# GpSimd's share of the square roots: a shorter iteration, and 40 pieces in place of 16

## The reference

```python
xn = _layernorm(x)
q2, k2 = sum(q * q), sum(k * k)
d2 = maximum(q2[..., :, None] + k2[..., None, :] - 2.0 * einsum('bhid,bhjd->bhij', q, k), 1e-12)
attn = softmax(-sqrt(d2), axis=-1)
out = einsum('bhij,bhjd->bhid', attn, v) @ wo.T + bo
```

## Time and profile before

| | |
|---|---|
| median of 3 runs | 1478.79 us (1478.11 to 1479.42) |
| profiled execution, its time | 1478.12 us |
| its span | 1476.4 us |
| ScalarE busy | 1445.5 us, 98% |
| VectorE busy | 1245.1 us, 84% |
| TensorE busy with matmuls | 1124.6 us, 76% |
| GpSimd busy | 632.1 us, 43% |
| mean granted TensorE clock | 0.935 |

### The profile page before, as it was taken

How to read it: one execution, slowest core, us unless ns; L and a number is a source line. 1 busy time by engine, 2 the same in 40 slices (tenths; PEclk the granted TensorE clock), 3 DMA queues, 4 the chain that set the end, 5 groups by cost and what they waited for, 6 DMA issues and landing times.

```text
span 1476.4 us, 21636 instructions
## 1 busy us (share of the span) xinstructions
PE 1124.6 (76%) x7910; PEld 439.8 (30%) x7910; DVE 1245.1 (84%) x2236; ACT 1445.5 (98%) x795; POOL 632.1 (43%) x529
## 2 busy tenths in 40 slices
PE   5587786887887988878879774787777677776766
PEld 2122223244242442442424410232123123221212
DVE  7897888988989889789798787858898898998886
ACT  4999999999999999999999999999999999999998
POOL 5166460755509577595685820732113024022200
PEclk8598888999999999999999997999999999999899
DMA  4842644223232212122121321034033133021020
GB/s 130 242 143 56 171 128 124 53 58 85 79 136 65 55 43 53 43 54 62 35 66 43 89 68 31 19 108 93 28 113 78 29 111 84 27 101 39 22 70 20
DMA packets 104062, 112.73 MB, mean 76 GB/s; under 512 B 41723, under 2 KB 76027, under 8 KB 103947
## 3 DMA queue, kind: packets, MB, share of 16 engines
q1 hardware_dynamic: 98618, 99.47, 24.8%
q0 software_dynamic: 4464, 11.09, 2.7%
q10 hardware_dynamic: 864, 0.69, 0.2%
HBM read 66.52 MB, written 44.70 MB: 75 GB/s over the span
## 4 chain that ended last, share of the span: by engine, by line
ACT 64%; DVE 13%; issue 13%; PE 7%; POOL 2%; DMA 1%; SPq 0%; DVEq 0%; ACTq 0%; POOLq 0%
ACT scores L776 25%; ACT scores L746 22%; ACT exp L1295 11%; DVE scores L695 6%; DVE exp L1303 4%; PE pvb L676 3%; ACT exp L1291 2%; PE ring L661 1%; ACT ht L1028 1%; ACT L776 1%; POOL yro L1082 1%; ACT L746 1%; PE ring L1270 1%; PE ring L989 1%; POOL at L1245 0%
## 5 line engine op out<-in xcount | busy, mean ns | idle before, releaser
L695 DVE TENSOR_SCALAR scores<-ring 128x1024 f32<-128x1024 f32 x512 | 589.2, 1212 | 27.3 <-PE ring L661 27.1
L776 ACT ACTIVATE scores<-scores 128x8192 f32<-128x8192 f32 x63 | 438.9, 7020 | 0.2
L1295 ACT ACTIVATE exp<-ring 128x1024 f32<-128x1024 f32 x438 | 432.6, 1416 | 0.2
L746 ACT ACTIVATE scores<-scores 128x8192 f32<-128x8192 f32 (+1 forms) x60 | 411.2, 6921 | 2.7 <-DVE scores L695 2.5
L1270 PE MATMUL ring<-stk 128*128 128x512 bf16 x1024 | 306.8, 386 | 122.1 <-ACT exp L1295 102.5
L676 PE MATMUL pvb<-scores,val 128*9 128x256 f32 x4096 | 325.2, 393 | 82.7 <-issue 39.1
L1303 DVE SCALAR_TENSOR_TENSOR exp<-exp 128x512 f32<-128x512 f32 x438 | 322.3, 757 | 61.0 <-ACT exp L1295 56.6
L661 PE MATMUL ring<-stk 64*128 64x512 bf16 x1024 | 209.9, 407 | 55.0 <-DVE scores L695 44.0
L1270 PEld LDWEIGHTS ring<-stk 128*128 128x128 bf16 x1024 | 65.8, 97 | 337.6 <-ACT exp L1295 240.5
L661 PEld LDWEIGHTS ring<-stk 64*128 64x128 bf16 x1024 | 49.8, 93 | 286.2 <-DVE scores L695 205.4
L676 PEld LDWEIGHTS pvb<-scores,val 128*9 128x9 f32 x4096 | 66.1, 89 | 213.3 <-issue 210.5
(11 more groups left out here) (262 smaller groups left out, 1402.8 us busy)
## 6 DMA issues: line engine op xcount, KB each, us to landing
stk<-stack SPq DMA_DIRECT2D x192, 192.0 KB, 2.9
stack<-qp SPq DMA_DIRECT2D x7, 768.0 KB, 4.6
stack<-kp SPq DMA_DIRECT2D x7, 768.0 KB, 5.6
xj<-xg SPq DMA_DIRECT2D x10, 448.0 KB
yg<-xj POOLq DMA_DIRECT2D x10, 448.0 KB, 3.6
stack<-qp SPq DMA_DIRECT2D x7, 512.0 KB, 5.2
stack<-kp SPq DMA_DIRECT2D x7, 512.0 KB, 5.1
stk<-sum_rows SPq DMA_DIRECT2D x128, 24.0 KB
```

The source lines that it names most:

```text
L695: nc.vector.tensor_scalar(S[place][:, j * N:(j + 1) * N], tile, 1e-12, None, ALU.max).then_inc(o.release(("qk", group, place, j)), 1)
L746: nc.scalar.activation(part, part, ACT.Sqrt).then_inc(root_done, 1)
L776: nc.scalar.activation(S[place][:], S[place][:], ACT.Exp, scale=-1.0).then_inc(exp_done, 1)
L1295: nc.scalar.activation(EX[k // 2][:, k % 2, :], tile, ACT.Exp, scale=SCALE1).then_inc(o.release(("qk1", n, i)), 1)
```

## The change

A piece on GpSimd now has the estimate (one instruction), one Newton step (four), and a last step of the third order: with a = x y and h = a y it forms ((0.375 h - 1.25) h + 1.875) a (six instructions). That makes 11 instructions for 14. Where there were 16 pieces of 448 columns, all at place 1, there are 40 at places 1 and 3:

| rounds | place 1 | place 3 |
|---|---|---|
| 2 | 1 | |
| 3 | 2 | 1 |
| 6 | 2 | 1 |
| 7 to 13, each | 3 | 1 |
| 14 | 2 | |
| 15 | 3 | |

ScalarE takes the root of what is left of the place, and waits for GpSimd ahead of the exponential of each of these places. GpSimd waits, ahead of each piece, for the tile of VectorE's that the piece ends in, and ahead of the first of a place for its own last root. The pieces of place 1 move behind placing, gathers, clears and scatters (ahead of the attention store), and those of place 3 stand behind the job store.

```diff
-NEWTON, NEWTON_PLACE = 448, 1
-NEWTON_ROUNDS = [7, 8, 9, 10, 11, 12, 13, 15]
+NEWTON, EARLY_PLACE, LATE_PLACE = 448, 1, 3
+NEWTON_PIECES = {(2, 1): 1, (3, 1): 2, (3, 3): 1, (6, 1): 2, (6, 3): 1}
+for newton_round in range(7, 14):
+    NEWTON_PIECES[newton_round, EARLY_PLACE] = 3
+    NEWTON_PIECES[newton_round, LATE_PLACE] = 1
+NEWTON_PIECES[14, EARLY_PLACE] = 2
+NEWTON_PIECES[15, EARLY_PLACE] = 3
+NEWTON_ORDER = list(NEWTON_PIECES)
...
-        def pool_roots(pool, o, chain, group):
-            o.emptied(pool, ("qk", group, NEWTON_PLACE, 0))
+        def pool_roots(pool, o, chain, group, place):
             y, h = root_y[:], root_h[:]
-            for i in range(2):
-                x = S[NEWTON_PLACE][:, i * NEWTON:(i + 1) * NEWTON]
+            pieces = NEWTON_PIECES.get((group, place), 0)
+            if pieces and NEWTON_ORDER.index((group, place)):
+                pool.wait_ge(newton_done, NEWTON_ORDER.index((group, place)))
+            for i in range(pieces):
+                end = (i + 1) * NEWTON
+                x = S[place][:, end - NEWTON:end]
+                o.emptied(pool, ("qk", group, place, (end - 1) // N))
...
-                for _ in range(3):
-                    chain.step(nc.gpsimd.tensor_tensor(h, x, y, ALU.mult))
...
+                chain.step(nc.gpsimd.tensor_tensor(x, x, y, ALU.mult))
+                chain.wait()
+                chain.step(nc.gpsimd.tensor_tensor(h, x, y, ALU.mult))
+                chain.wait()
+                chain.step(nc.gpsimd.tensor_scalar(y, h, 0.375, -1.25, ALU.mult, ALU.add))
+                chain.wait()
+                chain.step(nc.gpsimd.tensor_tensor(y, y, h, ALU.mult))
+                chain.wait()
+                chain.step(nc.gpsimd.tensor_scalar(y, y, 1.875, None, ALU.add))
+                chain.wait()
                 root = nc.gpsimd.tensor_tensor(x, x, y, ALU.mult)
...
-            part = S[place][:, 2 * NEWTON if by_newton(group, place) else 0:CH * N]
+            part = S[place][:, newton_columns(group, place):CH * N]
...
-            if by_newton(group, place):
-                act.wait_ge(newton_done, NEWTON_ROUNDS.index(group) + 1)
+            if newton_columns(group, place):
+                act.wait_ge(newton_done, NEWTON_ORDER.index((group, place)) + 1)
...
-                    if r in NEWTON_ROUNDS:
-                        pool_roots(pool, o, roots, r)
...
                     if r == PLACE_ROUND + 2:
                         pool_scatter(pool, 7)
+                    pool_roots(pool, o, roots, r, EARLY_PLACE)
                     if r:
                         pool_store_out(pool, r - 1)
...
                     if FIRST_JOBS < r <= LAST_JOBS + 1:
                         pool_store_jobs(pool, o, r - 1)
+                    pool_roots(pool, o, roots, r, LATE_PLACE)
```

More of the change, by code:

```diff
@@ L716, in pool_store_out, with newton_columns @@
                 pool.dma_start(dst, attg[:, 4 * t:4 * t + 4, :]).then_inc(att_out, 16)
-        def by_newton(group, place):
-            return group in NEWTON_ROUNDS and place == NEWTON_PLACE
-        def pool_roots(pool, o, chain, group):
-            o.emptied(pool, ("qk", group, NEWTON_PLACE, 0))
+        def newton_columns(group, place):
+            return NEWTON * NEWTON_PIECES.get((group, place), 0)
+        def pool_roots(pool, o, chain, group, place):
             y, h = root_y[:], root_h[:]
-            for i in range(2):
-                x = S[NEWTON_PLACE][:, i * NEWTON:(i + 1) * NEWTON]
+            pieces = NEWTON_PIECES.get((group, place), 0)
[5 more added lines that the diff above has]
+                o.emptied(pool, ("qk", group, place, (end - 1) // N))
@@ new lines, in pool_roots @@
+                chain.wait()
+                chain.step(nc.gpsimd.tensor_tensor(h, h, y, ALU.mult))
+                chain.wait()
+                chain.step(nc.gpsimd.tensor_scalar(h, h, -0.5, 1.5, ALU.mult, ALU.add))
+                chain.wait()
[3 more added lines that the diff above has]
+                chain.wait()
+                chain.step(nc.gpsimd.tensor_tensor(h, x, y, ALU.mult))
@@ L737, in pool_roots @@
+                chain.wait()
+                chain.step(nc.gpsimd.tensor_scalar(y, h, 0.375, -1.25, ALU.mult, ALU.add))
+                chain.wait()
+                chain.step(nc.gpsimd.tensor_tensor(y, y, h, ALU.mult))
+                chain.wait()
+                chain.step(nc.gpsimd.tensor_scalar(y, y, 1.875, None, ALU.add))
+                chain.wait()
                 root = nc.gpsimd.tensor_tensor(x, x, y, ALU.mult)
-                if i == 0:
+                if i < pieces - 1:
                     chain.step(root)
@@ L740, in pool_roots @@
                     chain.wait()
-            root.then_inc(newton_done, 1)
+                else:
+                    root.then_inc(newton_done, 1)
         def act_root(act, o, group, place):
             o.emptied(act, ("qk", group, place, CH - 1))
-            part = S[place][:, 2 * NEWTON if by_newton(group, place) else 0:CH * N]
+            part = S[place][:, newton_columns(group, place):CH * N]
             nc.scalar.activation(part, part, ACT.Sqrt).then_inc(root_done, 1)
```

## The result

The changed kernel takes 1482.35 us (median of 10 runs, 1481.71 to 1483.41) where the kernel before takes 1478.78 (10 runs): a ratio of 1.0024, 95% interval 1.0016 to 1.0032. It is 3.6 us slower. 1470.9 was forecast, 7.9 us faster, with 0.07 for any slowing. The profiled execution took 1482.24 us with a span of 1480.5. Of all executions reported here one stands out, one of E6's eleven with 3854 us: its interval leaves it out, and without it E6's median is 1477.78.

The account below looks back on a forecast made before the run. ScalarE's own work was taken to bound the kernel. 21 counting pieces at 0.375 us gave -7.9 from the profiled 1478.12, so 1470.2; the median of runs, 0.67 above, made 1470.9 us, range 1469.3 to 1475.9.

Parts of the forecast that it names:

- GpSimd: what a piece costs: Step pricing a new GpSimd piece at 11.16 us from instruction spacing, between bounds of 10.2 and 13.5.
- Rival B: GpSimd becomes the bound in rounds 7 to 13, lateness adding up; at 12.0 us a piece 1484.8 us; chance 0.07.
- 11.8 as the deciding price: GpSimd's price per piece, in us, from about which Rival B was said to decide.
- C's far end: Slowest time given for Rival C, 1475.9 us, taken as the upper end of the forecast range.
- the 13.5: Upper bound on a piece's us, all 11 instructions at the two-input price of 1.23; some 46 us slower.
- Spacing rather than spans: Pricing GpSimd instructions by start-to-start spacing, 11.16 us a piece, since recorded spans, giving 10.2, are called unreliable.
- 21 of the 24 pieces count: Of 24 added pieces, round 3's three are worth nothing; the others shorten ScalarE's roots by 21 x 0.375 = 7.9 us.
- the piece of round 2: Piece ahead of the exp that PE's values product waited for, so its 0.375 us is passed on to round 4.
- Rival A: PE and VectorE govern rounds 7 to 13, costing up to 2.9 us of the gain, 1473.8 us; chance 0.10.
- 4.4 us of cover: Time by which VectorE finishes a place before ScalarE's fourth root starts, round 9, once three pieces stand ahead.
- Rival C: VectorE and GpSimd block each other, notably round 3's late piece and choice of experts: 2 to 5 us; chance 0.05.
- Rivals D and E: First: all 24 pieces count, 1469.8 us, chance 0.06. Second: gain not passed on, within 3 us of before, 0.06.

Follow-up runs that it names:

- E6: Changed kernel, add of 1.875 written with two constants in the place 3 pieces only, one constant kept at place 1: 1477.89 us.
- E1: Changed kernel with the add of 1.875 written with two constants (times 1.0, plus 1.875) in every piece: 1470.70 us.
- E8: E1 without round 3's pieces, with two pieces at place 1 and one at place 3 in round 2, and one at place 3 in round 14: 1472.42 us.
- E2: Changed kernel, one-constant add kept, without the late piece at place 3 in rounds 7 to 13: 1474.23 us.
- E5: E1 without the three pieces of round 3: 1470.83 us.
- E4: Kernel before, plus GpSimd scalar instructions with one and two constants at 448 and 224 columns in round 14: 1477.78 us beside 1477.57.

## Why the prediction was wrong

**The step that failed** is "GpSimd: what a piece costs": "I take 11.16, as L726, a scalar instruction with two constants too, is the nearest row". Of the four scalar instructions of the new piece three have two constants, and for them that was right (565 ns); the fourth has one and took 1330. The step said that the new forms weren't in the trace. They were. Two constants on f32 is what each Newton step of before has (L733, 565 ns in the mean of 48). For one constant, from the groups of the kernel before by shape, ahead of round 0:

```profile
L1579 POOL TENSOR_SCALAR noise<-turns 128x256 f32<-128x256 f32 x3 | 2.6, 853 | 2.6 <-DVE sump L624 2.4
...
L1586 POOL TENSOR_SCALAR ang<-ang 128x128 f32<-128x128 f32 x1 | 0.5, 533 | 0.1
L1588 POOL TENSOR_SCALAR ang<-ang 128x256 f32<-128x256 f32 x1 | 0.4, 399 | 0.1
```

L1579 multiplies by one constant and L1586 adds one; L1588 has two (a minimum and a maximum). At 256 columns one constant takes 853 ns and two 399. From 128 to 256 columns one constant adds 320 ns, or 2.5 a column: 853 + 192 x 2.5 = 1333 at 448 (an estimate). Rows met only once or twice scatter: L1574, another add of one constant at 256 columns, took 992, and L1571, two constants at 128, 458. With 1333 the piece is 2.56 + 8.60 + 0.77 = 11.93, as measured.

**Rival B had the mechanism.** Put 11.93 into its own formula: a round of 13.6 + 47.7 = 61.3, 2.45 us more lateness each, 14.7 over six rounds less the 2.7 of cover = 12.0 lost against 7.9 won, 1482.9; 1482.35 was measured, with 11.1 lost. It was given 0.07 because "11.16 comes from like instructions whose spans vary by 0.01 us". The precision of a row says nothing for an instruction of another form, and with 0.6 us idle and 11.8 as the deciding price, 6% on the piece was all that stood between gain and loss. The range was bounded by C's far end and left out the 13.5 that the same text names as the upper bound.

**What held.** ScalarE's side: roots of 7744, 7296 and 6848 columns take 6.65, 6.27 and 5.90 us, the period is 58.87 (forecast 58.87), and with the piece's price mended the sum is right: E1 takes 1470.70 where 1470.9 was given. Spacing rather than spans: E1's 11.18 against 11.16 from spacing and 10.2 from spans. The two-constant forms, for which the whole piece was weighed between 10.2 and 13.5, lie where they were put.

That 21 of the 24 pieces count is shown for 20. ScalarE's timelines of before, of E1 and of the changed kernel, the table loads behind the roots of rounds 4 and 15:

```profile
305.25 1.28 ACT L776 ACT_TABLE_LOAD   x1
...
959.00 1.28 ACT L776 ACT_TABLE_LOAD   x1
```

```profile
305.17 1.28 ACT L798 ACT_TABLE_LOAD   x1
...
951.48 1.28 ACT L798 ACT_TABLE_LOAD   x1
```

```profile
305.12 1.28 ACT L798 ACT_TABLE_LOAD   x1
...
962.72 1.28 ACT L798 ACT_TABLE_LOAD   x1
```

Before takes 653.75 us for this stretch and E1 646.31: 7.4 us, for the 20 pieces that E1 has more in it (7.5 by the forecast). The stretch ahead of it, with the pieces of rounds 2 and 3, ends at 305.2 in both, and both begin round 2's roots at 158.0 to 158.1. So the piece of round 2, which was said to be passed on, shows no gain there; its 0.4 us is less than what executions differ by.

**Rival A** fell, but less clearly than its 4.4 us of cover suggested: in E1 the cover of the fourth root held in rounds 5 to 13, with 1.5 us left at the end. VectorE's and ScalarE's timelines in round 13 of E1, the end of place 3 and the end of the roots:

```profile
828.68 0.41 DVE L707 COPY ot<-pvb 128x256 f32<-128x256 f32 x1
```

```profile
836.91 1.28 ACT L798 ACT_TABLE_LOAD   x1
```

The fourth root (6.65 us) starts at 830.2, and VectorE is done with its place at 828.7. The loop fell back as the forecast said (0.7 to 2.9 us in seven rounds), near its upper end. In round 14, outside the rounds that rival A names, E6 and E8 do wait, 1.05 and 1.06 us.

**Rival C** came true in small. The late piece of round 3 ended at 251.87, where 250.6 was reckoned, and met the choice of experts. The changed kernel's timelines of GpSimd and of VectorE:

```profile
250.73 1.14 POOL L758 TENSOR_TENSOR scores<-scores,root_y 128x448 f32<-128x448 f32 x1
```

```profile
251.26 0.73 DVE L851 TENSOR_SCALAR odds<-odds 128x224 f32<-128x224 f32 x1
```

VectorE's first small instruction takes 0.27 us otherwise; here it starts inside GpSimd's last one and ends at 251.99, 0.12 after GpSimd's end at 251.87. In E1 that instruction takes 0.27 again. In E6 it takes 0.41 and ends at 252.99, where GpSimd ended at 252.85. In E2 it takes 1.17, over the 1 us that the forecast named as this rival's sign. The timelines of GpSimd and of VectorE in E2:

```profile
252.01 1.13 POOL L757 TENSOR_TENSOR scores<-scores,root_y 128x448 f32<-128x448 f32 x1
```

```profile
252.12 1.17 DVE L850 TENSOR_SCALAR odds<-odds 128x224 f32<-128x224 f32 x1
```

The rule that the forecast cited, for a VectorE instruction with two SBUF inputs, doesn't cover this one, which has one. The Trainium skill (SBUF — State Buffer, Who interferes with whom) says that a VectorE `tensor_scalar` can also run in a mode that takes the ports it shares with GpSimd, and that whoever issues first keeps them for the whole instruction while the other blocks; the three traces agree with the blocking, as VectorE ends 0.12 to 0.15 us after GpSimd each time, and which mode ran no trace shows. It lengthened that instruction by 0.5 us in the changed kernel and by 0.9 in E2. The VectorE instructions behind it begin after GpSimd's end and take what they take in E1.

**Rivals D and E** fell: without round 3's pieces E5 equals E1, and E1's span is 7.4 us shorter than that of before (1469.0 against 1476.4), as much as was won by round 15.

**The changed kernel's 3.6 us.** Waits of 10.6 and lost overlap of 0.5, less the 7.4 that E1's trace shows as won, are 3.7. In the trace the stretch between the two table loads takes 657.60 us, 3.85 more than before.

## What to carry to other kernels

When work moves to an engine until it is nearly full, the price of one instruction decides the sign: find a row of that engine with the same operation, the same number of constants and operands, wherever in the trace it stands, and scale it by size. Reckon the helper engine's round as a sum against the main engine's round; if it is longer, lateness adds up silently over rounds before the first wait shows. Ask of every rival at what price it decides, and how far that is from the price taken: a few per cent is not 0.07.

## What the hardware showed that was not expected

GpSimd's scalar instruction with one constant is slower than with two: 1.33 against 0.57 us at 128 x 448 f32 for add, multiply and maximum alike, and 0.78 against 0.38 at 224 for the add (E4). No run here shows why. Adding a second operation that does nothing (times 1.0) made the kernel 11.7 us faster.
